# Shared experts of three steps as jobs among the first attention's rounds, in a two-layer decoder kernel

## The chip, the cores and the metric

The kernel runs as one program on one core of a Trainium2 chip. The engines of a core are TensorE (PE; its weight loads are shown apart, as PEld), VectorE (DVE), ScalarE (ACT), GpSimd (POOL) and SyncE (SP), which here only issues DMAs. Each engine takes its own instructions strictly in the order in which the program gives them, and engines wait for each other through semaphores. The metric is the device time of one execution in microseconds (us), the median of several executions. All data are float32; the trace shows two matmul records for each matmul of the program.

## The reference

Two decoder layers over `x` [4, 1024, 256], each with a mixing attention, a cross attention on 77 context rows and an expert feed-forward, with a layer norm after each. What matters here is the feed-forward of the first layer: 64 routed experts of width 64, of which each token takes 8, and two shared experts of width 512 that every token takes:

```python
def body(acc, p):                       # 64 routed experts
    W1, B1, W2, B2, e = p
    h = jax.nn.silu(xf @ W1 + B1) @ W2 + B2
    cw = jnp.sum(jnp.where(ti == e, tw, 0.0), axis=-1)
    return (acc + cw[:, None] * h, None)
routed, _ = jax.lax.scan(body, jnp.zeros_like(xf), (w1, b1, w2, b2, jnp.arange(w1.shape[0])))

def shared_mlp(W1, B1, W2, B2):         # 2 shared experts
    return jax.nn.silu(xf @ W1 + B1) @ W2 + B2
shared = jnp.sum(jax.vmap(shared_mlp)(sw1, sb1, sw2, sb2), axis=0)
return (routed + shared).reshape(b_, s_, d_)
```

## The kernel before

The program has four phases one after the other: the attention of layer 0, the feed (the feed-forward of layer 0), the attention of layer 1 and the gated feed-forward of layer 1. The sequence of 1024 tokens is cut into 8 steps; a step is 128 tokens of each of the 4 batch rows, so 512 tokens.

**The first attention** is a software pipeline of rounds. `SEQUENCE0` is a list of (stage, ahead, part), and in round n the stage works on step n - ahead. So round n does the retention of step n (`v`, `qk`, `kt`, `ret`, `mix`, `up`), the cross attention of step n - 1 (`wo`, `x1t`, `mx`, `mt`, `sc`, `pv`), the router of step n - 2 (`wout`, `x2t`, `rt`, `top`, `rank`) and the last things of step n - 3 (`cwt`, `b2`, and `put`, which scatters the rows of the step into the lists of their experts). Rounds 0 to 7 have the retention, round 8 has only the rest, and rounds 9 and 10 the tail. All engines go through the same list of jobs. A job of PE fills one of four narrow PSUM banks in turn, or the one wide bank of four (`ret`, `mx`, `sc`), and another engine empties it: `filled` and `emptied` are the waits. The stages `ret`, `mx` and `sc` share the one wide bank, so each of them waits until the one before was emptied.

**The shared experts** are cut into units. A step has `UNITS` = 8 units (1024 hidden columns by 128), so there are 64. A unit is `inward` (two matmuls of 512 columns, line 110), `activate` (Silu on ScalarE, line 118) and `outward` (four matmuls of 256 columns, line 127, which add up over the 8 units of a step). Units 0 to 7 stand in rounds 9 and 10 (`with_units`), all others in the feed.

**The feed** follows `feed_order`: first 20 units (`FIRST_UNITS`), then 80 quads of four expert pages each, with units between them. A quad loads 512 KB of rows from `lists`, PE transposes them (line 1716), multiplies by W1 (line 1728) and W2 (line 1739), and 512 KB go to `results`. The first 24 quads (`begun`) hold all pages of step 0. From quad 24 on there is a unit in four of five quads, and a `sum` in six of seven from the 26th on:

```python
units(0 if (j - begun) % 5 == 0 else 1)
if j >= begun + 2 and (j - begun) % 7:
    sums(1)
```

A `sum` n is `add_up` on DVE: it waits for gather n, four indirect DMAs of POOL (line 1441) that fetch the rows of one of the eight experts of a step, and adds them to the step. POOL runs gathers 0 to 48 one after the other within the feed, each with a `rest` instruction (line 158) ahead of it, and the other 15 in the second attention. DVE also copies the weights of the next quad (`stage`, lines 1633 and 1638), in the same order: the copy for quad 79 stands in quad 78, behind the sums of the quads before. The sums 46 to 48 stand ahead of all that DVE does in the second attention.

`base` adds the shared experts' result of a step to its residual rows, and `send` stores them; 8 steps, so 8 of each.

Of the kernel before, what the change touches and what calls it, by code (L numbers as in the profile page):

```python
# [11 lines left out]
P = 128  # L12
# [20 lines left out]
TOTAL = STEPS * UNITS  # L33
# [44 lines left out]
class SharedExperts:  # L78
# [16 lines left out]
    def load_rows(self, sp, src_t, s):  # L95
        for b in range(NB):
            at = b * SEQ + s * P
            sp.dma_start(self.sx[:, s % 2, :, b * P:(b + 1) * P],
                         src_t[:, at:at + P].rearrange("(c p) n -> p c n", p=P)).then_inc(self.sx_in[s % 2], 16)

    def inward(self, nc, pe, n, sp_h):
        s, u = n // UNITS, n % UNITS
        if n == 0:
            pe.wait_ge(self.sw1_in, 16 * ES)
# [16 lines left out]
    def outward(self, nc, pe, n, sp_y):  # L121
        u = n % UNITS
        if n == 0:
            pe.wait_ge(self.sw2_in, 16)
# [40 lines left out]
def steady(sequence):  # L165

    order = []
    for n in range(STEPS + max(ahead for _, ahead, _ in sequence)):
        for stage, ahead, part in sequence:
            if 0 <= n - ahead < STEPS:  # L170
                order.append((stage, n - ahead, part))
    return order
# [31 lines left out]
def bank_jobs(order):  # L204
# [5 lines left out]
    ("wout", 2, 0), ("wout", 2, 1), ("cwt", 3, 0), ("put", 3, 1), ("qk", 0, 0), ("x1t", 1, 0), ("x1t", 1, 1),  # L210
# [17 lines left out]
def attention_phase(nc, sems, shared, layer, d, src, src_t, dst, dst_t, experts, prefetch, lists, slots, weights, page_ends,  # L228
                    spare=None, route=None, block=None,
                    over=(), kept=(), late_on_pool=None, late_on_vector=None, units=None):  # L230
# [17 lines left out]
    with ExitStack() as ctx:  # L248
# [61 lines left out]
        if first:  # L310
# [25 lines left out]
            qt = x1t  # L336
        else:
# [49 lines left out]
        if first:  # L387
            cw_done = sem("cw_done")
            sent_cols = sem("sent_cols")
            sent_place, sent_cw = sem("sent_place"), sem("sent_cw")  # L390
            blank = [sem(f"blank{i}") for i in range(STEPS)]
        else:
            gate_exp = sem("gate_exp")
            sig_done = sem("sig_done")
            comb_done = sem("comb_done")
# [60 lines left out]
        def _(sp):  # L456
# [23 lines left out]
            prefetch(sp, 0)  # L480
            if first:
                sp.wait_ge(pool_ready, 3)
            out_rows = dst.rearrange("(b s) n -> s b n", b=NB)
            for n in range(STEPS + 3 if first else 0):
# [3 lines left out]
                if n == 1:  # L488
                    sp.dma_start(units.sb1[:], d["sb1"]).then_inc(units.sb1_in, 16)
                if 0 <= n - 3 < STEPS:  # L490
# [15 lines left out]
                if n + 2 < STEPS:  # L506
                    filled(sp, ("v", n, 1))
                    filled(sp, ("qk", n, 3))
                    load_t(n + 2)
                if n == STEPS - 1:  # L510
# [7 lines left out]
                    sp.wait_ge(sent_cols, 64 * 2)  # L518
                    for k in range(2):
                        units.load_rows(sp, dst_t, k)  # L520
                if 0 <= n - 2 < STEPS:
                    sp.wait_ge(cw_done, n - 1)
                    sp.dma_start(route[n - 2, 1], cw[:].rearrange("p b e -> p (b e)")).then_inc(sent_cw, 16)
                    sp.wait_ge(slot_done, n - 1)
                    sp.dma_start(route[n - 2, 0], place[:].rearrange("p b e -> p (b e)")).then_inc(sent_place, 16)
            for n in range(0 if first else STEPS + 3):
# [88 lines left out]
        def _(act):  # L615
# [71 lines left out]
        def _(dve):  # L687
# [83 lines left out]
            for job in order:  # L771
# [151 lines left out]
                if stage == "rank":  # L923
# [50 lines left out]
        def _(pe):  # L974
# [35 lines left out]
            for job in order:  # L1010
# [219 lines left out]
                if stage == "rank":  # L1230
# [6 lines left out]
                    fills(ins, job)  # L1237
                if stage == "cwt":
# [10 lines left out]
        if first:  # L1249
# [3 lines left out]
            over += [(blank[k], 16 * len(blanks(k))) for k in range(STEPS)]  # L1253
            return over, put_of[:2], (slot_done, STEPS)
# [13 lines left out]
def feed_order():  # L1268
# [33 lines left out]
    for j in range(QUADS0):  # L1302
# [7 lines left out]
        else:  # L1310
            weights(1)
            units(0 if (j - begun) % 5 == 0 else 1)
# [11 lines left out]
def feed_phase(nc, sems, shared_sems, d, w1, w_in, lists, page_ends, results, slots, weights, last_x2, last_slots, src, src_t, dst,  # L1324
# [9 lines left out]
    with ExitStack() as ctx:  # L1334
# [84 lines left out]
        def load_base(pool, s):  # L1419
            pool.wait_ge(base_sent, 16 * (s + 1))  # L1420
# [79 lines left out]
        def _(sp):  # L1500
# [9 lines left out]
            def load_rows(s):  # L1510
                if s:
                    sp.wait_ge(base_sent, 16 * s)
                sp.dma_start(base, by_step[s * P:(s + 1) * P]).then_inc(base_in, 16)

            def send_base(s):
                sp.wait_ge(sy_used, s + 1)
                sp.dma_start(out_by_step[s * P:(s + 1) * P], base).then_inc(base_sent, 16)
# [15 lines left out]
            for kind, n in order:  # L1533
# [14 lines left out]
                if kind == "unit" and n and n % UNITS == 0 and shared < STEPS:  # L1548
# [3 lines left out]
                if kind == "send":  # L1552
                    send_base(n)
                    if n + 1 < STEPS:
# [7 lines left out]
            sp.wait_ge(base_sent, 16 * STEPS)  # L1562
# [207 lines left out]
        over = [(sent[n], 16 * len(range(n, QUADS, NY))) for n in range(NY)] + [(base_sent, 16 * STEPS)]  # L1770
# [327 lines left out]
def decoder(nc, a, out):  # L2098
# [19 lines left out]
    with ExitStack() as ctx:  # L2118
# [24 lines left out]
        with nc.Block() as block:  # L2143
            over, put_before, placed = attention_phase(
                nc, sems, shared, 0, layer0, a["x"], a["x_t"], res1, res1_t, E0, load_layer0, lists0, slots0, weights0, page_ends0,
                halves[1], route0, block, units=experts)
# [78 lines left out]
```

## Time and profile before

| | before |
|---|---|
| median of 3 runs | 1869.29 us (1869.01 to 1887.16) |
| span of the profiled execution | 1981.9 us |
| mean granted TensorE clock | 0.922 of full |
| busy, PE / DVE / ACT / POOL | 1687.5 / 1165.2 / 623.2 / 892.7 us |
| chain that ended last | PE 68%, DVE 10%, issue 6%, DMA 6%, ACT 4%, POOL 3% |
| first attention, rounds 0 to 8 | until 558 us |
| rounds 9 and 10 and the first 20 units of the feed | 558 to 685 us |
| quads 0 to 23 | 685 to 777 us |
| quads 24 to 79 | 777 to 1105 us |
| second attention | from 1129 us |

The profiled execution took 1981.9 us from its first to its last instruction, 6.0% over the median of the runs without a profile. The busy times are of the profiled execution. A busy PE says that its matmuls stand close to each other, not that the array is at its peak; the granted clock is the share of 2.4 GHz that it was given, and it has two levels, full (1.0) and half (0.5, 1.2 GHz).

### The profile page before, as it was taken

What the parts mean: (1) busy time and instruction counts of PE and PEld (TensorE: products, weight loads), DVE (VectorE), ACT (ScalarE), POOL (GpSimd) and SP (SyncE); (2) the same over time, 40 slices, a digit from 0 to 9 for tenths busy, and PEclk for the clock granted to TensorE, in tenths of its full rate; (3) what the DMA queues carried; (4) which work ended last, traced back from release to release, by engine and by line L of the source; (5) the groups of instructions that cost most, each with busy time, mean ns of one, the idle gap of its engine ahead of it and who ended that gap; (6) DMA issues with size and microseconds to landing.
All of it is one profiled execution on the core that took longest, in us unless ns stands there. A gap on an engine that the chain in (4) does not pass through costs nothing.

```text
span 1981.9 us, 45543 instructions
## 1 busy us (share of the span) xinstructions
PE 1687.5 (85%) x17739; PEld 1329.8 (67%) x17739; DVE 1165.2 (59%) x3228; ACT 623.2 (31%) x957; POOL 892.7 (45%) x1000
## 2 busy tenths in 40 slices
PE   6788888887689889998998478889977599999994
PEld 4566665666566567666676355667666499999994
DVE  4576655665432177776656456788765245655564
ACT  1232322222231277454555223445432111111110
POOL 0017556655758102888888856333323102222223
PEclk9999989998689999999998779999987699999997
DMA  9416543555448899888998922113111512333332
GB/s 325 150 46 199 184 150 116 190 169 191 146 147 237 219 304 295 285 278 273 297 294 290 317 78 82 57 65 121 69 39 65 164 49 76 91 94 98 98 94 69
DMA packets 269634, 322.61 MB, mean 163 GB/s; under 512 B 25083, under 2 KB 245487, under 8 KB 268655
## 3 DMA queue, kind: packets, MB, share of 16 engines
q1 hardware_dynamic: 234559, 226.38, 36.1%
q0 software_dynamic: 33024, 92.32, 14.4%
q8 instruction: 144, 2.36, 0.5%
q10 hardware_dynamic: 1840, 1.00, 0.2%
q14 instruction: 67, 0.55, 0.1%
HBM read 157.22 MB, written 162.40 MB: 161 GB/s over the span
## 4 chain that ended last, share of the span: by engine, by line
PE 68%; DVE 10%; issue 6%; DMA 6%; ACT 4%; POOL 3%; another core or an unknown queue 2%; SPq 1%; DVEq 1%; POOLq 0%; ACTq 0%
PE wide L2067 13%; PE d_yp L2079 6%; PE wide L110 4%; PE wide L127 4%; PE wide L1199 4%; PE wide L1202 3%; PE wide L1728 3%; PE e_yp L1739 3%; PE wide L1186 3%; PE bank L1033 3%; PE bank L1212 3%; PE bank L1219 2%; PE e_xp L1716 2%; PE bank L1105 2%
## 5 line engine op out<-in xcount | busy, mean ns | idle before, releaser
L1441 POOL DMA_INDIRECT big<-results,slots x256 | 263.4, 1029 | 202.1 <-DMA results<-e_y 125.5
L2067 PE MATMUL wide<-d_xt,d_ws 128*128 128x128 f32 x2272 | 279.0, 277 | 0.6 <-issue 0.6
L2067 PEld LDWEIGHTS wide<-d_xt,d_ws 128*128 128x128 f32 x2272 | 272.7, 193 | 4.5 <-issue 1.0
L597 POOL DMA_INDIRECT lists<-big,slots x160 | 159.6, 997 | 116.7 <-DVE slots L961 70.3
L663 ACT ACTIVATE pt<-wide 77x2048 f32<-77x2048 f32 x64 | 119.8, 1871 | 196.5 <-PE wide L1202 118.7
L1936 POOL DMA_INDIRECT d_picked<-results,slots x64 | 64.0, 1001 | 182.0 <-DMA results<-d_y 168.7
L1967 ACT ACTIVATE d_gate<-wide 128x512 f32<-128x512 f32 x71 | 42.4, 597 | 323.9 <-PE wide L2067 323.9
L2079 PE MATMUL d_yp<-d_wd,d_h 128*128 x568 | 134.2, 379 | 0.0
L1456 DVE SCALAR_TENSOR_TENSOR big<-big,weights 128x256 f32<-128x256 f32 x256 | 108.9, 487 | 41.6 <-DMA big<-results,slots 28.2
L110 PE MATMUL wide<-shared_sx,shared_sw 128*128 128x512 f32 x256 | 126.3, 616 | 7.7 <-DMA shared_sx<-res_t 5.2
L127 PEld LDWEIGHTS wide<-shared_sw,shared_sh 128*128 128x128 f32 x512 | 97.3, 191 | 45.1 <-issue 29.6
L127 PE MATMUL wide<-shared_sw,shared_sh 128*128 128x256 f32 x512 | 121.4, 380 | 3.6 <-DVE big L1697 3.6
L158 POOL TENSOR_TENSOR rest_ones<-rest_ones 128x4 f32<-128x4 f32 x108 | 121.0, 1120 | 2.0
L554 POOL TENSOR_TENSOR rs<-mv,eps 128x4 f32<-128x4 f32 x32 | 6.4, 199 | 234.9 <-DVE mv L712 234.1
L1212 PE MATMUL bank<-pt,vals 77*32 77x128 f32 x2048 | 89.6, 293 | 25.3 <-issue 15.4
L2079 PEld LDWEIGHTS d_yp<-d_wd,d_h 128*128 128x128 f32 x568 | 102.6, 190 | 11.0
L1998 DVE COPY d_ws<-big 128x1024 f32 x142 | 92.3, 693 | 27.5 <-issue 26.4
L2016 DVE TENSOR_TENSOR d_h<-d_gate,wide 128x512 f32<-128x512 f32 x71 | 48.7, 686 | 97.7 <-PE wide L2067 97.7
L1587 ACT ACTIVATE e_xt<-e_xp 128x1024 f32<-128x1024 f32 x80 | 81.9, 1024 | 76.5 <-PE e_xp L1716 48.7
L1716 PE MATMUL e_xp<-e_ident,e_x 128*128 128x128 f32 x640 | 86.9, 280 | 15.8 <-DMA e_x<-lists 12.2
L1199 PE MATMUL wide<-x1t,keys 32*77 32x128 f32 x1024 | 69.7, 315 | 35.8 <-issue 13.6
L1728 PE MATMUL wide<-e_xt,e_w1s 128*64 128x128 f32 x1280 | 89.4, 283 | 12.5 <-DVE e_w1s L1633 11.0
(280 smaller groups left out, 3488.8 us busy)
## 6 DMA issues: line engine op xcount, KB each, us to landing
lists<-zero SPq DMA_DIRECT2D x20, 2048.0 KB, 14.6
e_x<-lists SPq DMA_DIRECT2D x80, 512.0 KB
results<-e_y SPq DMA_DIRECT2D x80, 512.0 KB
d_x<-lists SPq DMA_DIRECT2D x71, 128.0 KB
results<-d_y SPq DMA_DIRECT2D x71, 128.0 KB
e_w<-in_L_w SPq DMA_DIRECT2D x2, 4096.0 KB
shared_sw<-in_x_t SPq DMA_DIRECT2D x32, 128.0 KB
x<-in_x SPq DMA_DIRECT2D x8, 512.0 KB
```

What stands on the lines that cost most here:

```text
L110: ins = nc.tensor.matmul(sp_h, self.sw1[:, c, u * P:(u + 1) * P], self.sx[:, s % 2, c], start=c == 0, stop=c == KC - 1)
L127: ins = nc.tensor.matmul(sp_y[b // 2][:, b % 2 * DM:(b % 2 + 1) * DM], self.sh[:, n % 2, b * P:(b + 1) * P], self.sw2[:, u], start=u == 0 ...
L158: step(self.nc.gpsimd.tensor_tensor(self.ones[:, 1], self.ones[:, 0], self.ones[:, 0], ALU.pow))
L597: pool.indirect_dma_start(out=lists, out_offset=bass.IndirectOffsetOnAxis(ap=slots[:, b, i, k:k + 1], axis=0), in_=z2[i % 3][:, b, :], in_ ...
L663: empties(nc.scalar.activation(pt[0:CTX, p % 2].rearrange("k (j n) -> k j n", j=4), ps[0:CTX], ACT.Exp, scale=score_scale), job)
L1199: mm(out[0:CTX, r, n * P:(n + 1) * P], keys[quarter(r), p, c, h * CTX:(h + 1) * CTX], qt[quarter(r), c, toks(p)], start=True, stop=False, ...
L1212: ins = mm(out[quarter(r), at:at + P], vals[:, p, c * 8 + 2 * r + h], pt[0:CTX, p % 2, of:of + P], start=True, stop=True)
L1441: pool.indirect_dma_start(out=picked[:, c % NG, b, :], out_offset=None, in_=results[0:-(-PAGES_OF_STEP[s] // 4) * 4 * R0, :], in_offset=ba ...
L1716: ins = tr(xp[:, h, (a * KC + c) * P:(a * KC + c + 1) * P], x[:, j % NX, h, a, c * P:(c + 1) * P], ident[:])
L1728: ins = mm(hp[h * H0:(h + 1) * H0, a * R0:(a + 1) * R0], w1s[:, j % NW1, h, a, c], xt[:, j % 2, h, a, c], start=c == 0, stop=c == KC - 1)
L2067: ins = mm(out[T % 2][:, a * P:(a + 1) * P], ws[:, T % NW, n, c, a * P:(a + 1) * P], xt[:, T % 2, c], start=c == 0, stop=c == KC - 1)
L2079: ins = mm(yp[T % 2][:, 0:DM], h[:, T % 2, c * P:(c + 1) * P], wd_flat[:, bass.ds(e * (HC * DM) + c * DM, DM)], start=c == 0, stop=c == HC ...
```

## The change

The shared experts of steps 0 to 2 (`SOON` = 3), 24 of the 64 units, become jobs of the first attention. A step is two groups of four units (`FOUR`); group i stands in round i + 3, so rounds 3 to 8 have one group each. A group is four jobs `win` (two matmuls of 512 columns each on PE; Silu on ScalarE) and two jobs `wtwo` (eight matmuls of 256 columns each on PE, which add up over the four units; DVE adds the bank to the residual rows `gbase`). The jobs use the narrow banks. The feed and `with_units` work on the other five steps, with 40 units: 8 in rounds 9 and 10, 20 at the start of the feed as before, and 13 instead of 37 between the quads, one in four quads.

```diff
+SOON = 3
+FOUR = UNITS // 2
+GROUPS = SOON * UNITS // FOUR
+TOTAL = (STEPS - SOON) * UNITS
...
-    ("wout", 2, 0), ("wout", 2, 1), ("cwt", 3, 0), ("put", 3, 1), ("qk", 0, 0), ("x1t", 1, 0), ("x1t", 1, 1),
+    ("wout", 2, 0), ("wout", 2, 1), ("cwt", 3, 0), ("put", 3, 1), ("win", 3, 0), ("qk", 0, 0), ("x1t", 1, 0), ("x1t", 1, 1),
...
-            units(0 if (j - begun) % 5 == 0 else 1)
+            units(0 if (j - begun) % 4 else 1)
...
+                if stage == "win":
+                    u, at = i % 2 * FOUR + p, i % 2 * FOUR + p
+                    if i == 0 and p == 0:
+                        act.wait_ge(units.sb1_in, 16)
+                    if i >= 2 and p == 0:
+                        filled(act, ("wtwo", i - 2, 1))
+                    ps = filled(act, job)
+                    empties(nc.scalar.activation(gh[:, at], ps[:], ACT.Silu, bias=units.sb1[:, u:u + 1]), job)
...
+                if stage == "wtwo":
+                    pair = slice(2 * p, 2 * p + 2)
+                    dve.wait_ge(gbase_in, 16 * (i // 2 + 1))
+                    ps = filled(dve, job)
+                    if i % 2:
+                        emptied(dve, ("wtwo", i - 1, p))
+                    ins = nc.vector.tensor_tensor(gbase[:, pair], ps[:].rearrange("p (b n) -> p b n", b=2),
+                                                  gbase[:, pair], ALU.add)
+                    empties(ins, job)
...
+                if stage == "win":
+                    u = i % 2 * FOUR + p
+                    if i == 0 and p == 0:
+                        pe.wait_ge(units.sw1_in, 16 * ES)
+                        pe.wait_ge(units.sw2_in, 16)
+                    if i % 2 == 0 and p == 0:
+                        pe.wait_ge(gx_in, 64 * (i // 2 + 1))
+                    for c in range(KC):
+                        ins = mm(out[:], gw1[:, c, u * P:(u + 1) * P], gx[:, c], start=c == 0, stop=c == KC - 1)
+                    fills(ins, job)
+                if stage == "wtwo":
+                    for n in range(FOUR):
+                        emptied(pe, ("win", i, n))
+                    for bb in range(2):
+                        for n in range(FOUR):
+                            u = i % 2 * FOUR + n
+                            ins = mm(out[:, bb * DM:(bb + 1) * DM], gh[:, u, toks(2 * p + bb)], gw2[:, u],
+                                     start=n == 0, stop=n == FOUR - 1)
+                    fills(ins, job)
```

On SP's queue the change adds, in the first attention: the shared experts' weights a second time, into the half of `big` that later holds the feed's W1 (in round 1, 2 MB), the step's columns `gx` (512 KB in rounds 2, 4 and 6, after the wait for `sent_cols`), the residual rows `gbase` (512 KB in rounds 3, 5 and 7, after the wait for `sent_rows`) and their store into `mid` (rounds 4, 6 and 8, after `wtwo` was emptied). The load of the feed's W1 (`prefetch`, 4 MB) moves from the start of the kernel to the end of round 8, and the first rows of the units in the tail from round 7 to round 8. The feed has 5 bases, 5 sends and 3 loads of unit rows where it had 8, 8 and 6. POOL's instructions are the same; only its wait for the stored base falls away for the first three steps.

In PE's order of round 6, from the transposed router weights (`cwt`) to `b2`, there stands before:

```order
L1241 MATMUL bank_0<-ident,cw 64x128 x4
L1033 MATMUL bank_0<-shared_sw,wqk 128x512 x2
L1105 MATMUL bank_0<-ident,x 128x128 x8
L1186 MATMUL wide<-keys,x1t 128x154 x8
L1033 MATMUL bank_0<-shared_sw,wqk 128x512 x2
L1246 MATMUL bank_0<-b_0,cwt 128x256 x4
```

and in the changed kernel:

```order
L1327 MATMUL bank_0<-ident,cw 64x128 x4
L1313 MATMUL bank_0<-big 128x512 x2
L1100 MATMUL bank_0<-shared_sw,wqk 128x512 x2
L1172 MATMUL bank_0<-ident,x 128x128 x8
L1253 MATMUL wide<-keys,x1t 128x154 x8
L1100 MATMUL bank_0<-shared_sw,wqk 128x512 x2
L1313 MATMUL bank_0<-big 128x512 x2
L1332 MATMUL bank_0<-b_0,cwt 128x256 x4
```

The first `win` stands ahead of the first `qk`, the second behind the second `qk`; the third stands behind the third `mx` and the fourth ahead of the first `kt`. Later in the same round, from the last matmuls of `mix` 0 over `ret` 1 (wide) and `pv` 0 to `sc` 1, before:

```order
L1074 MATMUL bank_0<-big,shared_sx 32x128 x4
L1057 MATMUL wide<-shared_sw 128x128 x16
L1212 MATMUL bank_0<-pt,vals 32x128 x16
L1199 MATMUL wide<-x1t,keys 77x128 x4
L1202 MATMUL wide<-shared_sh,sel 77x128 x4
```

and in the changed kernel:

```order
L1141 MATMUL bank_0<-big,shared_sx 32x128 x4
L1124 MATMUL wide<-shared_sw 128x128 x16
L1279 MATMUL bank_0<-pt,vals 32x128 x16
L1321 MATMUL bank_0<-big 128x256 x8
L1266 MATMUL wide<-x1t,keys 77x128 x4
L1269 MATMUL wide<-shared_sh,sel 77x128 x4
```

The second `wtwo` stands between `pv` 0 and `sc` 1; the first one stands in the same way between `sc` 0 and `mix` 0. On ScalarE, the same round, from `cwt` to the exponential of the router, in the changed kernel (before there is neither a Silu nor a table load in it):

```order
L667 ACTIVATE cwt<-bank_0 64x512
L687 ACT_TABLE_LOAD
L687 ACTIVATE big<-bank_0,shared_sb 128x512
L667 ACTIVATE x1t<-bank_0 128x2x2x128 x2
L740 ACTIVATE big<-big,rs 128x256 x4
L687 ACTIVATE big<-bank_0,shared_sb 128x512
L667 ACTIVATE x2t<-bank_0 128x2x2x128 x2
L687 ACTIVATE big<-bank_0,shared_sb 128x512 x2
L667 ACTIVATE shared_sx<-bank_0 128x512 x2
L667 ACTIVATE shared_sh<-bank_0 128x512
L725 ACT_TABLE_LOAD
L725 ACTIVATE ex<-lg 128x256
```

Silu and the exponential lie in different tables, so each of rounds 3 to 8 has two loads of a table on ScalarE, 12 in all.

## Rows read from the trace of the kernel before

**Rows 1.** The page: span, and the granted clock in 40 slices

```profile
span 1981.9 us, 45543 instructions
PEclk9999989998689999999998779999987699999997
```

**Rows 2.** Busy time by stretch: round 6, round 8, first units, quads in three stretches

```profile
core 0: us, PE busy (x) PEld busy (x) DVE busy (x) ACT busy (x) POOL busy (x), PEclk, DMA share, GB/s
350.50:417.80 67.30, 56.76 (x835) 42.96 (x831) 41.55 (x104) 18.67 (x25) 40.39 (x46) 0.92 0.48 156
485.00:558.40 73.40, 53.10 (x537) 39.78 (x534) 34.24 (x98) 15.40 (x19) 47.10 (x52) 0.68 0.61 202
600.40:685.20 84.80, 75.14 (x257) 48.28 (x255) 12.66 (x37) 14.43 (x21) 43.74 (x46) 0.96 0.89 233
685.20:776.60 91.40, 81.78 (x832) 62.47 (x832) 65.77 (x219) 67.65 (x103) 0.00 (x0) 1.00 0.92 294
776.60:1059.40 282.80, 268.88 (x1877) 191.21 (x1873) 183.66 (x599) 141.74 (x216) 229.31 (x219) 0.99 0.88 283
1059.40:1105.00 45.60, 34.79 (x298) 26.25 (x296) 30.74 (x110) 23.45 (x37) 37.57 (x37) 0.89 0.91 297
```

**Rows 3.** PE in order of time, units at the start of the feed

```profile
614.25 1.88 PE L110 MATMUL wide<-shared_sx,shared_sw 128*128 128x512 f32 x4
615.96 1.89 PE L127 MATMUL wide<-shared_sw,shared_sh 128*128 128x256 f32 x8
617.69 1.88 PE L110 MATMUL wide<-shared_sx,shared_sw 128*128 128x512 f32 x4
```

**Rows 4.** Waits of PE in round 6: us in total, times, longest

```profile
PE wide L1199 <- issue: 2.3, 3, 1.7
PE wide L1057 <- issue: 1.5, 2, 0.9
...
PE wide L1199 <- DVE big L788: 1.1, 1, 1.1
PE bank L1212 <- ACT pt L663: 1.1, 1, 1.1
```

**Rows 5.** Waits of PE in round 8

```profile
PE bank L1105 <- ACT x L674: 4.2, 2, 3.8
PE wide L1199 <- ACT pt L663: 3.4, 1, 3.4
...
PE bank L1212 <- ACT pt L663: 2.2, 2, 2.1
PE bank L1192 <- DVE shared_sh L854: 1.9, 1, 1.9
PE wide L1186 <- DVE shared_sh L854: 1.6, 1, 1.6
```

**Rows 6.** Waits of POOL from 780 to 1128 us

```profile
POOL big L1441 <- issue: 46.0, 151, 0.3
POOL big L1441 <- POOL rest_ones L158: 14.1, 49, 0.3
POOL big L1441 <- DVE big L1456: 0.3, 1, 0.3
```

**Rows 7.** POOL in order of time: two puts of four, gathers 0 and 48

```profile
631.59 1.04 POOL L1572 DMA_INDIRECT lists<-big,slots  x1 [0.29 <-POOL rest_ones L158]
...
637.77 1.04 POOL L1572 DMA_INDIRECT lists<-big,slots  x1 [0.29 <-POOL rest_ones L158]
...
780.61 0.99 POOL L1441 DMA_INDIRECT big<-results,slots  x1 [125.49 <-DMA results<-e_y]
...
1113.07 1.01 POOL L1441 DMA_INDIRECT big<-results,slots  x1 [0.29 <-POOL rest_ones L158]
```

**Rows 8.** DVE in order of time: sums 44 and 48, start of the second attention

```profile
1095.55 1.67 DVE L1456 SCALAR_TENSOR_TENSOR big<-big,weights 128x256 f32<-128x256 f32 x4 [2.14 <-issue]
...
1125.96 1.67 DVE L1456 SCALAR_TENSOR_TENSOR big<-big,weights 128x256 f32<-128x256 f32 x4 [5.36 <-DMA big<-mid]
1127.64 0.28 DVE L722 MEMSET state<- 128x260 f32 x1
```

**Rows 9.** ScalarE at the first unit, a load of the table and a Silu

```profile
566.20 1.28 ACT L118 ACT_TABLE_LOAD   x1 [9.80 <-PE wide L110]
567.50 0.69 ACT L118 ACTIVATE shared_sh<-wide,shared_sb 128x512 f32<-128x512 f32 x1
```

More of the change, by code:

```diff
@@ L169, in steady @@
         for stage, ahead, part in sequence:
-            if 0 <= n - ahead < STEPS:
+            if 0 <= n - ahead < (GROUPS if stage in ("win", "wtwo") else STEPS):
                 order.append((stage, n - ahead, part))
@@ L209 @@
     ("wo", 1, 0), ("wo", 1, 1), ("put", 3, 0), ("v", 0, 0), ("v", 0, 1), ("ln1", 1, 0),
-    ("wout", 2, 0), ("wout", 2, 1), ("cwt", 3, 0), ("put", 3, 1), ("qk", 0, 0), ("x1t", 1, 0), ("x1t", 1, 1),
[4 rows of a table removed]
+    ("wout", 2, 0), ("wout", 2, 1), ("cwt", 3, 0), ("put", 3, 1), ("win", 3, 0), ("qk", 0, 0), ("x1t", 1, 0), ("x1t", 1, 1),
+    ("mx", 1, 0), ("ln2", 2, 0), ("qk", 0, 1), ("win", 3, 1), ("b2", 3, 0), ("b2", 3, 1), ("mx", 1, 1), ("res", 1, 0), ("put", 3, 2),
+    ("qk", 0, 2), ("x2t", 2, 0), ("x2t", 2, 1), ("mx", 1, 2), ("win", 3, 2), ("put", 3, 3), ("qk", 0, 3), ("mx", 1, 3), ("put", 3, 4),
+    ("win", 3, 3), ("kt", 0, 0), ("ret", 0, 0), ("kt", 0, 1), ("put", 3, 5), ("mt", 1, 0), ("rt", 2, 0), ("put", 3, 6), ("put", 3, 7),
+    ("sc", 1, 0), ("wtwo", 3, 0), ("mix", 0, 0), ("top", 2, 0), ("ret", 0, 1), ("pv", 1, 0), ("wtwo", 3, 1), ("sc", 1, 1),
+    ("mix", 0, 1), ("up", 0, 0),
     ("rank", 2, 0), ("sc", 1, 2), ("pv", 1, 1), ("sc", 1, 3), ("pv", 1, 2), ("pv", 1, 3),
@@ L229, in attention_phase @@
                     spare=None, route=None, block=None,
-                    over=(), kept=(), late_on_pool=None, late_on_vector=None, units=None):
+                    over=(), kept=(), late_on_pool=None, late_on_vector=None, units=None, soon_memory=None, mid=None):
     first = layer == 0
@@ L479, in _, with load_group, load_gbase, send_gbase @@
             load_t(1)
-            prefetch(sp, 0)
             if first:
                 sp.wait_ge(pool_ready, 3)
+            else:
+                prefetch(sp, 0)
             out_rows = dst.rearrange("(b s) n -> s b n", b=NB)
+            def load_group(s):
+                for b in range(NB):
+                    at = b * SEQ + s * P
+                    sp.dma_start(gx[:, :, b * P:(b + 1) * P],
+                                 dst_t[:, at:at + P].rearrange("(c p) n -> p c n", p=P)).then_inc(gx_in, 16)
+            def load_gbase(s):
+                sp.wait_ge(sent_rows[0], 16 * (s + 1))
+                if s:
+                    sp.wait_ge(gbase_sent, 16 * s)
+                else:
+                    sp.wait_ge(ready, READY)
+                sp.dma_start(gbase, out_rows[s * P:(s + 1) * P]).then_inc(gbase_in, 16)
+            def send_gbase(s):
+                for p in range(2):
+                    emptied(sp, ("wtwo", 2 * s + 1, p))
+                sp.dma_start(mid.rearrange("(b s) n -> s b n", b=NB)[s * P:(s + 1) * P], gbase)\
+                    .then_inc(gbase_sent, 16)
             for n in range(STEPS + 3 if first else 0):
@@ L489, in _ @@
                     sp.dma_start(units.sb1[:], d["sb1"]).then_inc(units.sb1_in, 16)
+                    sp.dma_start(gw2, d["sw2"].rearrange("e (c p) n -> p (e c) n", p=P)).then_inc(units.sw2_in, 16)
+                    for e in range(ES):
+                        sp.dma_start(gw1[:, :, e * HS:(e + 1) * HS], d["sw1"][e].rearrange("(c p) n -> p c n", p=P))\
+                            .then_inc(units.sw1_in, 16)
                 if 0 <= n - 3 < STEPS:
@@ L509, in _ @@
                     load_t(n + 2)
+                if n >= 2 and n % 2 == 0 and n // 2 - 1 < SOON:
+                    s = n // 2 - 1
+                    if s:
+                        filled(sp, ("win", 2 * s - 1, FOUR - 1))
+                    sp.wait_ge(sent_cols, 64 * (s + 1))
+                    load_group(s)
+                if n >= 3 and n % 2 == 1 and (n - 3) // 2 < SOON:
+                    load_gbase((n - 3) // 2)
                 if n == STEPS - 1:
@@ L525, in _ @@
                     sp.dma_start(route[n - 2, 0], place[:].rearrange("p b e -> p (b e)")).then_inc(sent_place, 16)
+                if n >= 4 and n % 2 == 0 and n // 2 - 2 < SOON:
+                    send_gbase(n // 2 - 2)
+                    if n // 2 - 2 == SOON - 1:
+                        filled(sp, ("wtwo", GROUPS - 1, 1))
+                        prefetch(sp, 0)
             for n in range(0 if first else STEPS + 3):
@@ L1547, in _ @@
                     load_route((n + 1) // 6)
-                if kind == "unit" and n and n % UNITS == 0 and shared < STEPS:
+                if kind == "unit" and n and n % UNITS == 0 and SOON + shared < STEPS:
                     sp.wait_ge(experts.full, n)
@@ L1769, in feed_phase @@
         kept = [(stored[s % NA], 16 * (s // NA + 1)) for s in range(STEPS)]
-        over = [(sent[n], 16 * len(range(n, QUADS, NY))) for n in range(NY)] + [(base_sent, 16 * STEPS)]
+        over = [(sent[n], 16 * len(range(n, QUADS, NY))) for n in range(NY)] + [(base_sent, 16 * (STEPS - SOON))]
         return over, kept, late_on_pool, late_on_vector
```

30 lines of the change are left out of this document (19 added, 11 removed), and 4 rows, old and new, of the table SEQUENCE0.

## The prediction

> **What bounds the kernel now.** I read the busy times by stretch first, since the change takes work out of one stage and puts it into another, and then in each of the two stages which wait ends last. In the first attention a middle round takes 67.3 us and PE is busy for 56.8 of them; DVE has 41.6, POOL 40.4 and ACT 18.7 [rows 2]. The waits of PE in that round are many and small, the longest 1.7 us [rows 4]. So a round is as long as PE's own work with some 10 us of holes, of which only few are places where a foreign job would stand. Round 8 is different: no retention, 73.4 us long, PE busy for 53.1, clock 0.68 [rows 2], and waits of 4.2, 3.4, 2.2, 1.9 and 1.6 us on ACT and DVE [rows 5]. Round 8 follows from chains, and PE has room in it.
>
> In the feed the reader is to look at POOL, though PE is busier. From 776.6 to 1059.4 us PE is busy for 268.9 of 282.8 us [rows 2], which by itself says that PE bounds it. But POOL, whose busy time is only 229.3, has not one real wait in the whole stretch: its waits are 46.0 us before indirect DMAs and 14.1 us behind its own rest instruction, all of 0.3 us each, and a single 0.3 us for DVE [rows 6]. So POOL goes at its own pace from gather 0 at 780.61 to gather 48 at 1113.07 [rows 7], 332.5 us for 48 gathers, 6.93 us each. And the end of the feed hangs on it: DVE stood still for 2.14 us before sum 44 (which the program's order places ahead of the copies for the last quads) and for 5.36 us before sum 48 (on the residual rows, whose load POOL issues behind gather 48), and the second attention's first DVE instruction comes right behind that, at 1127.64 [rows 8]. From 1059.4 on, without a unit in the way, PE is busy for only 34.8 of 45.6 us [rows 2]: there the quads already follow POOL.
>
> **The change part by part.** *PE work put into the rounds.* A unit in full stride takes 617.69 - 614.25 = 3.44 us [rows 3], so a group of four 13.8 us, and six groups 82.6 us. The matmuls are the same in number and shape as in the feed.
>
> *Rounds 3 to 7.* What fills holes: the fourth `win` stands ahead of the first `ret`, and the first `wtwo` ahead of `mix` 0 and so of the second `ret`; the two waits of line 1057 (1.5 us) go. The second `wtwo` stands ahead of `sc` 1; the longest wait of line 1199 (1.7 us) goes [rows 4]. The waits of 1.1 us at the first `sc` and the last `pv` have no new job ahead of them and stay. That hides 3.2 us. Then the clock: 0.92 over 67.3 us [rows 2] means 16% of the round at half speed, 10.8 us, which would have taken 5.4 us at full speed. No trace shows what denser work does to it. The ends: all is given back (growth 13.8 - 3.2 - 5.4 = 5.2 us a round), or the half-speed stretch stays and one `wtwo` pair of 3.4 us falls into it and takes twice as long (13.8 - 3.2 + 3.4 = 14.0 us). I take 2 us given back, nearer to nothing than to all, because the jobs stand at two points of a stretch whose other matmuls stay as they are: 8.6 us a round, 43 us for five rounds, with ends of 26 and 70.
>
> *Round 8.* The first `win` stands ahead of the transposes that wait 4.2 us, the third ahead of the last `mx` (1.6), the fourth ahead of `mt` (1.9), the first `wtwo` ahead of `pv` 0 (2.2) [rows 5]: 9.9 of 13.8 us are hidden. The 3.9 left I set against the clock, which was at half speed for 64% of the round: 0, with ends of -10 and +8.
>
> *ScalarE and VectorE in the rounds.* 24 Silus of 0.69 us and 12 table loads of 1.28 us [rows 9] are 32 us, 5.3 a round on an engine that has 18.7 of 67.3 busy [rows 2]; the copies of `x1t` are queued behind the first Silu and PE's `mx` waits for them, but a `qk` of two 512-column matmuls and eight transposes lie between. The second table load lies ahead of the exponentials, for which the first `wtwo` gives PE 3.4 us of other work. Two DVE adds of about 0.7 us (as line 1456 takes 1.67 for four of half the size [rows 8]) lie in an idle DVE; `top` and `pv` are queued behind them, and PE has `mix` and `sc` to do meanwhile. I take 0; if each round showed the table load and the Silu once it would be 6 x 2.0 = 12 us.
>
> *SP's queue.* The waits for `sent_cols` and `sent_rows` stand ahead of the route stores, which wait for later work anyway; the wait for `wtwo` stands ahead of the next round's clears of the lists. The 4 MB load of W1 now lies at the end of round 8 instead of at the start. The DMA engines are 0.61 busy in round 8 [rows 2], and W1 is not needed before the first quad at 685 us; at 283 GB/s [rows 2] it takes 15 us. What can be late is the clear of the last part of the lists behind it. I take 0, with ends of -3 (the start is rid of it) and +8.
>
> *The feed.* 24 x 3.44 = 82.6 us of PE work go out of quads 24 to 79, three bases and sends with them. The first 20 units stay, and quads 0 to 23 (91.4 us, no units, DMA engines 0.92 busy [rows 2]) stay. What is late next is POOL, which is late already. Its pace could rise if less contends with it: two puts of four with their rest are 637.77 - 631.59 = 6.18 us apart [rows 7], so 48 gathers at that pace would take 297 us, 36 less than now; but every eighth gather also has a load, a store and two norm instructions on POOL, some 3 us, 18 us in all, which leaves 18 at most. The routed traffic of the quads and gathers, which fills the DMA engines to 0.88, is unchanged, so I take -3, with ends of 0 and -18.
>
> Sum: 43 + 0 + 0 + 0 - 3 = +40 us on the profiled 1981.9 us [rows 1], so 2022. The runs without a profile are at 1869.29, 0.943 of that, and the same share of the 40 is 38: 1907 us.
>
> **The rivals.** *The rounds swallow the jobs.* The granted clock is 1.00 where work stands dense (quads 0 to 23) and 0.92 and 0.68 in the rounds [rows 2]. If the added dense matmuls hold it at full speed, rounds 3 to 7 grow by 26 us, round 8 shrinks by 10 and the feed gives 3: +13 us, 1881. The Trainium skill (TensorE: Matmul & The Clock Gate, "What's actually happening") says that the default state is throttled and that activity releases the throttle; by that rule this rival wins, and the trace agrees in part, for round 8 has the lowest clock and the most idle PE. Against it speaks that the dips in rounds 3 to 7 lie where PE is 84% busy.
>
> *The feed gives PE's time back.* If POOL only looks busy because it is paced by the quads, quads 24 to 79 shrink by up to 82.6 us, and the kernel ends at 1981.9 + 43 - 83 = 1942, which is 1832 without a profile. For it speaks PE's 268.9 of 282.8; against it that POOL has no wait for sums or results. It comes out ahead by 1% only if gathers come every 6.93 - (43 + 20) / 48 = 5.6 us, less than the 6.18 that POOL needs where nothing disturbs it.
>
> *The rounds pay in full.* Half-speed stretches stay, the jobs run into them, table loads show, the last clear is late: 70 + 8 + 12 + 8 = 98 us, with the feed's 3 it is 95, 1959 us.
>
> **How the numbers follow.** Likeliest case 0.56 (its own range 1888 to 1930), the rounds swallow it 0.20, the feed gives back 0.09, pay in full 0.15. The range reaches from the second case with the feed's larger end (26 - 10 - 18 = -2, so 1867) to inside the last: 1867 to 1948. About 1% is what a measurement of this kernel can tell from no change, so 1850.6 and 1888.0 are the limits: faster 0.09, no difference 0.21 (the second case and the edge of the first), slower 0.70.
>
> **What would show it.** Right: rounds 3 to 7 some 76 us long each (67.3 before) and round 8 near 73; first gather of POOL late by the attention's growth; from there 332 us again to gather 48, still without waits, while PE is busy for about 190 of the 283 us and its clock falls there; the second attention and the gated phase unchanged in length. Wrong in the first step: rounds of 72 us or less at a clock of 1.0. Wrong in the last: gathers closer than 6.5 us. Also wrong if DVE waits for `gbase` in a round, or if the feed starts late behind W1.

## Result and the profile after

The changed kernel takes 1920.56 us (median of 4 runs, 1915.56 to 1922.53), the kernel before 1871.61 us: a ratio of 1.0256 with a 95% interval of 1.022 to 1.0293, so it is 2.6% slower. The forecast was 1907, range 1867 to 1948.

The first profile of the kernel before [rows 1 to 9] turned out to be of a disturbed execution: a second one (e1, below) has a span of 1866.4 us, close to its runs, so e1 stands for before from here on. Against e1 the first profile is 80.1 us longer up to the end of POOL's last put, 5.8 from there to quad 0 and 30.6 behind gather 48, all ahead of the gated feed-forward (421 us in both); from quad 0 to gather 48 it is 1.1 us shorter.

The page of e1, span and granted clock in 40 slices:

```profile
span 1866.4 us, 45543 instructions
...
PEclk9999999997999999999997689899985999999997
```

The page of the changed kernel:

```profile
span 1920.2 us, 45608 instructions
...
PEclk9999999999999898888998679999996899999997
```

The clock digits of the first attention (slices 1 to 11) are 9 in both but for one 7 in e1 (round 8), where [rows 1] have a 6 and two 8s. A 9 stands for anything from 0.90 on, so whether a round has 0.92 or 1.00 is read from the stretches below. By places that both traces have (the first `mx` of a round, POOL's last put, the first quad, the last gather of the feed), in us:

| stretch | before (e1) | after | difference |
|---|---|---|---|
| start to `mx` of round 3 | 162.4 | 161.0 | -1.4 |
| `mx` of round 3 to `mx` of round 8 | 273.3 | 323.5 | +50.2 |
| from there to the end of the last put | 139.1 | 138.0 | -1.1 |
| last put to quad 0 | 24.5 | 29.3 | +4.8 |
| quad 0 to gather 48 | 429.0 | 431.6 | +2.6 |
| gather 48 to the end | 838.2 | 836.8 | -1.4 |

The sum is 53.7 us between the two profiled executions, 49 between the medians. Rounds 3 to 7 hold nearly all of it. The other differences are about what executions of the same program differ by: from the last put to quad 0, for one, the changed kernel takes 29.3 us here, 26.2 in e4 and 26.7 in e9, whose programs are the same there but for the Silu of e4, and the kernel before 24.5 in e1, 26.5 in e12 and 29.4 in e10.

Busy time by stretch of e1, as in [rows 2]: round 5, quads 0 to 23, and gather 0 to quad 72. (The 91.4 us in [rows 2] run past quad 24, which begins at 767.4 us there; quads 0 to 23 take 82.2 us in both profiles.)

```profile
core 0: us, PE busy (x) PEld busy (x) DVE busy (x) ACT busy (x) POOL busy (x), PEclk, DMA share, GB/s
269.60:324.00 54.40, 48.59 (x832) 38.44 (x831) 41.88 (x104) 18.89 (x25) 39.93 (x46) 1.00 0.60 200
...
599.30:681.50 82.20, 72.48 (x736) 55.26 (x736) 57.73 (x191) 59.80 (x91) 0.00 (x0) 1.00 0.91 292
...
694.20:980.00 285.80, 274.01 (x1944) 196.32 (x1942) 190.15 (x611) 149.95 (x224) 235.69 (x223) 0.99 0.89 287
```

The same of the changed kernel, up to quad 77:

```profile
core 0: us, PE busy (x) PEld busy (x) DVE busy (x) ACT busy (x) POOL busy (x), PEclk, DMA share, GB/s
287.50:352.30 64.80, 62.40 (x880) 47.32 (x879) 42.83 (x105) 23.98 (x31) 40.86 (x46) 1.00 0.57 185
...
651.80:734.70 82.90, 74.20 (x738) 56.28 (x736) 59.77 (x198) 59.93 (x91) 0.00 (x0) 0.98 0.92 292
...
747.70:1050.00 302.30, 224.44 (x1762) 165.28 (x1762) 198.67 (x652) 140.71 (x213) 249.21 (x235) 0.87 0.84 273
```

The reader is to see two things. A round gained 62.40 - 48.59 = 13.81 us of PE work and became 10.4 us longer; its holes shrank from 5.81 to 2.40 us, and the clock was full in both. In the feed PE went from 274.0 of 285.8 us to 224.4 of 302.3, and the time from gather 0 to gather 48 did not shrink. In e1 and in the changed kernel (POOL in order of time, start and us, as in [rows 7]):

```profile
694.20 0.99 POOL L1441 DMA_INDIRECT big<-results,slots  x1 [119.23 <-DMA results<-e_y]
...
1028.25 1.01 POOL L1441 DMA_INDIRECT big<-results,slots  x1 [0.29 <-POOL rest_ones L158]
```

```profile
747.67 0.99 POOL L1529 DMA_INDIRECT big<-results,slots  x1 [124.97 <-DMA results<-e_y]
...
1083.37 1.01 POOL L1529 DMA_INDIRECT big<-results,slots  x1 [0.29 <-POOL rest_ones L161]
```

That is 334.1 and 335.7 us. Which holes were filled, the waits of PE show, as [rows 4] did. In e1's round 5 (us in total, times, longest):

```profile
PE wide L1199 <- DVE big L788: 2.4, 1, 2.4
PE bank L1212 <- ACT pt L663: 1.1, 1, 1.1
PE wide L1199 <- ACT pt L663: 1.0, 1, 1.0
PE wide L1057 <- DVE shared_sh L854: 0.8, 1, 0.8
PE wide L1186 <- ACT x1t L617: 0.3, 1, 0.3
```

and in the changed kernel's round 5:

```profile
PE bank L1279 <- ACT pt L721: 1.1, 1, 1.1
PE wide L1266 <- ACT pt L721: 1.0, 1, 1.0
PE wide L1253 <- ACT x1t L667: 0.3, 1, 0.3
```

The 2.4 us ahead of `sc` 1 (line 1199) and the 0.8 us ahead of `ret` (line 1057) are gone, 3.2 us; the other three stand as they were.

### The profile page after: what moved, and what is told of

The parts are those of the page before. It is cut to its first block, busy times and chain, and to the rows that moved or that the text cites. A ratio compares the mean times of both kernels' runs of the same rounds, so it can differ in the third digit from the quotient of the medians.

```text
span 1920.2 us, 45608 instructions
## 1 busy us (share of the span) xinstructions
PE 1631.4 (85%) x17739; PEld 1300.8 (68%) x17739; DVE 1171.6 (61%) x3234; ACT 639.4 (33%) x969; POOL 898.5 (47%) x1000
## 4 chain that ended last, share of the span: by engine, by line
PE 59%; POOL 18%; issue 7%; DVE 7%; DMA 5%; ACT 4%; SPq 1%; DVEq 0%; POOLq 0%; ACTq 0%
PE wide L2155 13%; POOL big L1529 11%; PE d_yp L2167 6%; POOL rest_ones L161 3%; PE bank L1100 3%; PE wide L1266 3%; PE wide L1269 2%; PE bank L1286 2%; PE bank L1313 2%; PE bank L1321 2%; PE wide L1253 2%; PE wide L113 2%; PE wide L130 2%; ACT pt L721 2%; PE bank L1279 2%
## 5 line engine op out<-in xcount | busy, mean ns | idle before, releaser
L1816 PE MATMUL wide<-e_xt,e_w1s 128*64 128x128 f32 x1280 | 99.5, 304 | 81.0 <-DVE e_w1s L1721 80.8
L1816 PEld LDWEIGHTS wide<-e_xt,e_w1s 128*64 128x64 f32 x1280 | 77.8, 151 | 96.9 <-DVE e_w1s L1721 89.1
L1827 PE MATMUL e_yp<-e_w2s,e_ht 64*128 64x256 f32 x640 | 105.1, 453 | 1.3 <-ACT e_y L1675 1.3
L1804 PE MATMUL e_xp<-e_ident,e_x 128*128 128x128 f32 x640 | 89.2, 284 | 13.1 <-DMA e_x<-lists 11.5
L1675 ACT ACTIVATE e_y<-e_yp 128x1024 f32<-128x1024 f32 x80 | 81.9, 1024 | 54.6 <-PE e_yp L1827 54.6
L1804 PEld LDWEIGHTS e_xp<-e_ident,e_x 128*128 128x128 f32 x640 | 71.9, 144 | 39.3 <-DMA e_x<-lists 20.4
L658 POOL DMA_INDIRECT lists<-shared_sw,slots x64 | 62.4, 975 | 70.0 <-PE wide L1269 30.4
```

Source lines behind the costliest of these rows:

```text
L1675: return nc.scalar.activation(out, in_, ACT.Copy)
L1804: ins = tr(xp[:, h, (a * KC + c) * P:(a * KC + c + 1) * P], x[:, j % NX, h, a, c * P:(c + 1) * P], ident[:])
L1816: ins = mm(hp[h * H0:(h + 1) * H0, a * R0:(a + 1) * R0], w1s[:, j % NW1, h, a, c], xt[:, j % 2, h, a, c], start=c == 0, stop=c == KC - 1)
L1827: ins = mm(yp[:, h, a * DM:(a + 1) * DM], ht[lanes, j % 2, a], w2s[lanes, j % NW2, a, 0:DM], start=True, stop=True)
```

## The experiments

Three theories. A, the prediction's: the rounds pay for the jobs, since PE bounds them, and the feed gives next to nothing back, since POOL paces it. B: the feed does give PE's time back, 30 us or more, and the rounds pay 80. C: the added loads, stores and waits on SP's queue pay part of it.

**e1, the kernel before again.** No edit.

> The kernel before, unchanged, for a second profile: the span of the first one (1981.9 us) lies 6% over its runs without a profile, while the span of the changed kernel (1920.2 us) lies at its runs. If the recording itself costs 6%, the span is near 1980 again. If the first profile held stretches that most executions don't have, the span is near 1870, the gathers of the feed keep their pace of 6.9 us, and the rounds of the first attention are shorter than 67.3 us: near 57 if theory A is right (each round pays some 8 us for its group; the changed kernel's are 64.8).

The span was 1866.4 us, and the second case holds: the rounds are 54.4 us long, not 67.3. The recording itself costs nothing that shows. The clock of 0.92 explains 5.4 of the 12.9 us by which a round of the first profile is longer. Most of the rest shows as waits of PE that nothing in the profile ends ("issue"), mostly between its matmuls of 32 rows or 32 columns: 31.7 us from round 3 to round 7 in the first profile (148.2 to 485 us), 0.9 us in e1 (148.2 to 433 us). What caused them is open.

**e2, no jobs.** `win` and `wtwo` leave the list; SP waits for its own loads instead.

```diff
-    ("sc", 1, 0), ("wtwo", 3, 0), ("mix", 0, 0), ("top", 2, 0), ("ret", 0, 1), ("pv", 1, 0), ("wtwo", 3, 1), ("sc", 1, 1),
+    ("sc", 1, 0), ("mix", 0, 0), ("top", 2, 0), ("ret", 0, 1), ("pv", 1, 0), ("sc", 1, 1),
...
-                    emptied(sp, ("wtwo", 2 * s + 1, p))
+                sp.wait_ge(gbase_in, 16 * (s + 1))
```

> The changed kernel with the jobs win and wtwo left out on PE, ScalarE and VectorE (the shared experts of steps 0 to 2 are computed nowhere); its loads and stores, the place of the load of W1 and the short feed stay. Theory A (the rounds pay, the feed is paced by POOL and gives some 3 us back): 1865 to 1872 us, at the kernel before or up to 5 us under it. Theory B (the feed gives 30 us or more back and the rounds pay 80): 1840 or less. Theory C (the new loads, stores and waits on SP pay part of the 49 us): 1885 or more.

1874.06 us, ratio to before 0.9998 (0.9979 to 1.0018). With the loads, the stores, the late W1 and the short feed all in place the kernel is as fast as before: the 49 us are the jobs, and C falls as an explanation of them. A's 1865 to 1872 was missed by 2 us. C is not nothing, though, as e3 shows.

**e3, the short feed alone.**

```diff
-TOTAL = STEPS * UNITS
+SOON = 3
+TOTAL = (STEPS - SOON) * UNITS
...
-            units(0 if (j - begun) % 5 == 0 else 1)
+            units(0 if (j - begun) % 4 else 1)
```

> The kernel before with the changed kernel's short feed: 24 units left out between the quads (the shared experts of steps 0 to 2 are computed nowhere), nothing else moved. What the feed alone gives back. Theory A: 0 to 5 us under the kernel before, gathers again 6.8 to 6.9 us apart and without waits. Theory B: 30 us or more under it, gathers 6.2 us apart or less.

1866.96 us, ratio 0.9949 (0.9932 to 0.9965), 7 us under before by the medians and 10 by the ratio. 82.6 us of PE work are gone, and 7 to 10 us come back. B falls, and A's 0 to 5 was too little. Gather 0 to gather 48 takes 335.0 us, no less than before:

```profile
698.76 0.99 POOL L1444 DMA_INDIRECT big<-results,slots  x1 [123.29 <-DMA results<-e_y]
...
1033.78 1.01 POOL L1444 DMA_INDIRECT big<-results,slots  x1 [0.29 <-POOL rest_ones L159]
```

Where the 7 us lie the profiles don't tell; the profiled execution of e3 was the slowest of its four. Neither e2 nor e3 has the jobs, both have the short feed, and what e2 has beyond e3 are the loads, the stores, their waits and the late W1. It is 7 us slower (1874.06 against 1866.96), and the two intervals don't overlap: C's part costs about what the short feed gives back. In which stretch is not shown.

**e4, no table loads.**

```diff
-gh[:, at], ps[:], ACT.Silu, bias=units.sb1[:, u:u + 1]
+gh[:, at], ps[:], ACT.Identity, bias=units.sb1[:, u:u + 1]
```

> The changed kernel with Identity in place of Silu for the jobs win (so the result of the shared experts of steps 0 to 2 is another one), which takes the 12 table loads out of rounds 3 to 8. If ScalarE's table loads lie beside other work, as the prediction took it: 1915 to 1921 us, within 5 us of the changed kernel. If each round shows its table load and a Silu: 12 us less, near 1908.

1916.81 us, ratio 1.0231 (1.0208 to 1.0254), which overlaps the changed kernel's interval. The rounds are the same to 0.1 us; round 5 of e4:

```profile
290.70:355.50 64.80, 62.40 (x880) 47.33 (x879) 42.86 (x105) 21.40 (x29) 40.82 (x46) 1.00 0.56 183
```

ScalarE is busy for 21.40 instead of 23.98 us, and nobody notices: its work lies beside PE's. The feed is the changed kernel's, and its gathers 0 to 48 take 331.4 us here and 335.7 there: single profiles of the same code differ by 4 us in that stretch.

**e5, fewer units ahead of the first quad, in the changed kernel.**

```diff
-FIRST_UNITS = 20
+FIRST_UNITS = 12
...
-            units(0 if (j - begun) % 4 else 1)
+            units(1 if (j - begun) % 5 in (1, 3) else 0)
```

> The changed kernel with 12 instead of 20 units ahead of the first quad and 20 instead of 13 between quads 24 to 79 (two in five). If the feed is paced by POOL and has PE time to spare since the change (in the changed kernel PE is busy for 73 to 79 of each 100 us there), the eight units cost nothing between the quads, and the first quad follows the last put of POOL after some 8 us instead of 29: about 20 us less than the changed kernel, near 1900. If PE's time in the feed still counts, the 27 us only move: near 1920.

1919.56 us, ratio 1.0254 (1.0214 to 1.0295): nothing. The first quad began at 641.54 instead of 651.82 us, 10 us earlier and not 20, and PE stood still for 23.8 us ahead of it. SP's queue in order of time (start, us) shows why:

```profile
602.25 24.27 SPq L101 DMA_DIRECT2D shared_sx<-res_t  x4
626.56 2.17 SPq L1605 DMA_DIRECT2D mid<-big  x1
636.02 0.36 SPq L1601 DMA_DIRECT2D big<-res  x1
636.49 7.38 SPq L1592 DMA_DIRECT2D e_x<-lists  x4
```

The rows of the first quad (`e_x`) are queued behind the next `base` load, and that waits until the stored base has landed, 9 us. POOL's last put had ended at 623.8. Of the 10 us that were gained, 4 are left at the end of the profile: the gathers took 339.9 instead of 335.7 us and quads 0 to 23 1.6 us more, both within what single profiles of the same code differ by. The medians show 1.

**e6, the same in the kernel before**, with `units(1 if j % 8 == 7 else 0)` for quads 0 to 23.

> The kernel before with the same 12 units ahead of the first quad, three units between quads 0 to 23 and 44 between the others. Here PE has less room: in the second profile of the kernel before it is busy for 103.2 of 105.8, 92.6 of 100 and 78.2 of 80 us between gather 0 and quad 72. If POOL alone paces the feed: 16 to 20 us under the kernel before. If PE is a close second, as those numbers say, the gathers go some 2 to 4% slower (7.1 us apart) and half or more of it is lost: 5 to 10 us under.

1878.04 us, ratio 1.0029 (0.9998 to 1.006): a miss. Quad 0 starts 11.5 us earlier than in e1 (587.8 against 599.3), but quads 0 to 23 with three units take 91.5 instead of 82.2 us, and the gathers 339.9 instead of 334.1:

```profile
587.80:679.30 91.50, 84.09 (x760) 63.72 (x760) 58.24 (x190) 61.31 (x93) 0.00 (x0) 0.94 0.82 263
...
694.40:980.00 285.60, 275.96 (x1917) 196.31 (x1916) 187.12 (x606) 147.66 (x222) 236.28 (x218) 0.99 0.90 289
```

Before the change PE is a close second limit in the feed. In quads 0 to 23 the three units of 3.44 us show nearly in full (9.3 us); of the five more among the gathers, 17.2 us of PE work, 5.8 us show.

**e7, one step, its groups in rounds 7 and 8**, 12 units ahead of the first quad.

```diff
-SOON = 3
+SOON = 1
...
-    ("win", 3, 3), ("kt", 0, 0), ("ret", 0, 0), ("kt", 0, 1), ("put", 3, 5), ("mt", 1, 0), ("rt", 2, 0), ("put", 3, 6), ("put", 3, 7),
+    ("win", 7, 3), ("kt", 0, 0), ("ret", 0, 0), ("kt", 0, 1), ("put", 3, 5), ("mt", 1, 0), ("rt", 2, 0), ("put", 3, 6), ("put", 3, 7),
```

> The changed kernel with one step instead of three (SOON = 1), its two groups in rounds 7 and 8, and 12 units ahead of the first quad, so that the eight units come out of the stretch that bounds the first quad. By the readings so far a group costs 10.4 us in a round with retention (64.8 against 54.4 us) and nothing in round 8: 10.4 - 20 = 10 us under the kernel before, near 1864. If round 8 was free only by chance of the long rounds ahead of it: near 1874.

1875.41 us, ratio 1.002 (0.9995 to 1.0044): no gain, and a miss. From `cwt` of round 7, which stands ahead of the first job, to the end of the last put it takes 206.6 us (196.8 in e1), 9.8 us for two groups, as 10.4 and nothing would give. The time fits the other case of the expectation, near 1874, but its reason doesn't hold: from `mx` of round 8 to the last put it takes 138.3 us, and 139.1 in e1, so round 8 is free here too. The gain at the first quad is missing for e5's reason: PE waited 25.9 us for `e_x`, whose load followed that of the `base` at 599.05 us.

**e8, one step, both groups in round 8.** The list is rewritten so that `win` and `wtwo` of both groups stand in round 8 alone.

> As the one ahead, but both groups stand in round 8, which has no retention. PE is busy for 58.8 of the 73 us from round 8's start in the second profile of before, at a clock of 0.86, so there are some 14 us of holes and a group is 13.8 us: the first is free, the second costs between 0 and 13.8 us there. 1854 to 1868; under the one ahead if the holes take more than 3 us of the second group, which is what a round with retention takes.

1879.36 us, ratio 1.0044 (1.0019 to 1.0068), slower than before: a miss. Round 8 did what was expected of it, for the last put ends 5.8 us later than in e1 (580.66 against 574.82) with 27.6 us of PE work more. But PE then waits for SP's queue:

```profile
602.86 1.51 PE L1804 MATMUL e_xp<-e_ident,e_x 128*128 128x128 f32 x6 [24.17 <-DMA e_x<-lists]
```

**e9 and e10, half of POOL's rests**, in the changed kernel and in the kernel before.

```diff
-            if c:
+            if c and (c % 2 or c >= LATE):
                 shared_sems.rest(pool)
```

> The changed kernel, with POOL's rest instruction ahead of every second of the gathers 1 to 45 instead of ahead of every one (23 rests of some 1.33 us with their wait fall away, 31 us). If POOL's own pace sets the feed (theory A): gathers 6.3 instead of 7.0 us apart, 25 to 31 us less than the changed kernel, 1890 to 1895. If the gathers only look busy and go at the pace of the quads, of DVE or of the DMA engines: they wait in other places, the time stays at 1915 to 1921.

> The same in the kernel before, where PE is busy for 274 of the 285.8 us from gather 0 to quad 72. Theory A with PE as the second limit: PE's time holds the gathers back, so it gains only what PE has spare and the part after the last unit, 8 to 16 us under the kernel before, 1856 to 1864, and the distance to the changed kernel with the same edit shrinks from 49 to some 35 us. If PE had been no limit at all: 25 to 31 us under, 1841 to 1847, and the distance stays. If POOL is not the limit: no change.

e9: 1896.56 us, ratio 1.0155 (1.0096 to 1.0215), 24 us under the changed kernel by the medians and 2 above its range (the rests taken away are 22, not 23: 29 us). Gather 0 to gather 48 takes 310.6 us, 25.1 less:

```profile
743.80 0.99 POOL L1529 DMA_INDIRECT big<-results,slots  x1 [120.04 <-DMA results<-e_y]
...
1054.40 1.01 POOL L1529 DMA_INDIRECT big<-results,slots  x1 [0.29 <-POOL rest_ones L161]
```

e10: 1863.06 us, ratio 0.9944 (0.9918 to 0.997). Gather 0 to gather 48 takes 321.5 us, only 12.5 less, and POOL now waits (us in total, times, longest):

```profile
POOL big L1441 <- issue: 53.2, 164, 3.8
POOL big L1441 <- POOL rest_ones L158: 6.9, 24, 0.3
POOL mid L1417 <- DVE big L1477: 6.1, 2, 4.5
POOL big L1441 <- DVE big L1456: 5.6, 2, 5.3
```

Waits of 5.3 and 4.5 us for DVE's sums and norms stand where [rows 6] have none over 0.3. Both halves of A are shown by this pair: POOL's own instructions set the feed, and the PE time that the change takes out becomes worth something (12 us here) when POOL goes faster. That PE stands behind DVE's delay in e10 is an inference, from PE's 274.5 of 281.8 us between gather 0 and 980 us. The distance between the kernels falls from 49 to 33.5 us.

**e11 and e12, a third of the rests**: e11 with e8's round 8, 20 units ahead of the first quad and 28 between the quads (`units((j - begun) % 2)`); e12 is the kernel before with nothing else.

```diff
-            if c:
+            if c and (c % 3 == 0 or c >= LATE):
                 shared_sems.rest(pool)
```

> A version meant to beat both: one step (SOON = 1) as two groups in round 8 as in e8, 20 units ahead of the first quad as before, 28 between the quads (every second), and a rest ahead of every third of the gathers 1 to 45 (30 rests fewer, 40 us). Round 8 costs 6 us by e8's profile, PE in the feed has nine units or 31 us less to do than before. If POOL's pace sets the feed as long as PE has time: gathers 6.1 us apart, 6 - 38 = 32 us under the kernel before, near 1838, with PE near full. If the gathers have a third limit (DVE's sums, landing): 1850 to 1863, no better than e10.

> The kernel before with the same third of the rests, no unit moved. If PE already bounds the feed of e10 (gathers 6.7 us apart, PE busy for 278.7 of 286 us): nothing more is gained, 1860 to 1866, and the units moved to round 8 in e11 are worth the difference, some 25 us. If it gains as much as e11 (under 1845), PE is not the limit and moving units is worth nothing even with a faster POOL.

e11: 1863.78 us, ratio 0.995 (0.9918 to 0.9982); 1838 was a miss. e12: 1856.31 us, ratio 0.9897 (0.9865 to 0.9928), the fastest kernel of all and 4 us under its range. In e11 the gathers go as expected, 299.2 us from the first row to the second, 6.2 us each, and POOL's longest wait among them is 0.3 us:

```profile
714.43 0.99 POOL L1529 DMA_INDIRECT big<-results,slots  x1 [130.06 <-DMA results<-e_y]
...
1013.58 1.01 POOL L1529 DMA_INDIRECT big<-results,slots  x1 [0.29 <-POOL rest_ones L161]
```

In e12 they take 319.7 us, hardly less than in e10, with PE at 273.2 of 281.3 us:

```profile
698.70:980.00 281.30, 273.23 (x1935) 195.60 (x1933) 189.81 (x618) 148.99 (x223) 208.21 (x201) 0.99 0.90 293
```

So the units moved out do buy 20.5 us in the gathers. They are lost on both sides of them. Quad 0 of e11 starts at 615.6 us, that of e12 at 603.0 (7.7 us of it in the attention, the rest behind the last put). And the end of the gathers no longer decides: gather 48 starts 4.8 us earlier in e11, but PE begins the second attention 7.7 us later, at 1039.01 against 1031.28 us, having waited 24.9 us (22.3 in e12) for constants that SP loads behind the last quad's store. In e11 that store is late because of the units, of which the last still stand behind the last quad:

```profile
1007.60 1.14 PE L1827 MATMUL e_yp<-e_w2s,e_ht 64*128 64x256 f32 x8 [1.27 <-ACT e_y L1675]
1008.67 1.98 PE L113 MATMUL wide<-shared_sx,shared_sw 128*128 128x512 f32 x4
1010.49 3.62 PE L130 MATMUL wide<-shared_sw,shared_sh 128*128 128x256 f32 x16
```

DVE waits 9.9 us for them before the last `base`, SP 7.7 us for DVE before it stores that base, and the last quad's store is queued behind it: the second attention's first load starts at 1021.08 us, in e12 at 1015.98, though the last quad's last matmuls start at 1007.60 and 1007.89. From gather 0 to 980 us the DMA engines are busy at a share of 0.96:

```profile
714.40:980.00 265.60, 243.72 (x1824) 176.56 (x1823) 193.29 (x639) 143.18 (x217) 213.09 (x205) 0.95 0.96 313
```

Why e12 is 7 us under e10, whose gathers take as long, is open; their intervals overlap.

## Why the prediction held, point by point

**The rounds are bound by PE and pay** (right, mis-sized). 13.8 us of PE work a group and 3.2 us of filled holes, as forecast: 13.81 and 3.2 were measured. The holes are at the two places that were named, but that their sum agrees is luck: 1.7 us ahead of `sc` 1 and 1.5 ahead of `ret` in the disturbed profile are 2.4 and 0.8 in e1. The step that was off is the clock: 2 us a round were to be given back, because the first profile showed 0.92. In e1 and in the changed kernel the clock is 1.00 in round 5, so there was nothing to give back, and a round grew by 10.4 us, not 8.6: 50 instead of 43. For the same reason the prediction's own sign of a wrong first step came, rounds of 72 us or less at a clock of 1.0 (64.8 at 1.00), without the step being wrong: the rounds before are not 67.3 us long but 54.4.

**Round 8 costs nothing** (right): -1.1 us from its `mx` to the last put.

**ScalarE, VectorE and SP cost nothing in the rounds** (right): e4 for the table loads, e2 for the loads and stores (its round 5 takes 54.5 us), and no wait of DVE for `gbase` in any round. Over the whole kernel SP's part was taken as 0, with ends of -3 and +8, and e2 against e3 puts it at some 7. The Trainium skill (ScalarE: Activation LUTs, "What ACT_TABLE_LOAD costs") gives 2.66 us for a switch, 1.28 of load and 1.38 of drain. This trace shows the load alone: in round 4 the instruction ahead of it ends at 221.73 us, the load starts at 221.75 and takes 1.28, and the Silu follows at 223.04. That it doesn't count for the time e4 shows.

**The feed is paced by POOL and gives 3 us back** (right in kind). The profiles show +2.6 from quad 0 to gather 48, which is no clear difference, e3 by its runs -7. PE was to be busy for some 190 of 283 us; from gather 0 to gather 48 it was busy for 239.2 us instead of 301.0, only 61.8 less for 82.6 us of work taken out, since the clock fell from 0.99 to 0.87, as forecast. The first quad is 4.8 us later behind the last put, which the sum had at 0: PE waited 6.8 us for the rows of a unit there (2.0 in e1), behind SP's queue. Other executions of both kernels differ by as much there.

**From the profile to the median** (wrong): the sum was multiplied by 0.943, as if those 6% lay everywhere. They lay nearly all in the two attentions. In hindsight, without that factor and the clock term the same working gives 5 x (13.8 - 3.2) - 3 = 50 us, 1919 on the median it started from; the measured time is 1920.56.

**The rivals.** That the rounds swallow the jobs fell with the full clock of e1. That the feed gives PE's time back fell with e3, and its condition (gathers under 5.6 us apart) was never met, not even with a third of the rests (6.2). That the rounds pay in full came nearest, but its half-speed stretches and table loads are not there.

## What to carry to other kernels

A busy engine is not the pace of a stage. In this feed PE was 96% busy and POOL 82%, yet taking 82.6 us from PE gave 7 to 10 us back, and taking 29 us from POOL (22 rests of 1.33) gave 24: look for the engine that has no wait, however its busy time reads. Before work is moved, ask of both places what bounds them; here it went from under POOL's cover into the one stage that PE did bound. And compare a profile's span with the unprofiled runs by stage before a sum is scaled from one to the other.

## What the runs showed of the hardware

The clock of TensorE dropped where its work became thinner. From gather 0 on it was at 0.99 with PE busy for 274 of 285.8 us, and at 0.87, so in part at the lower level of 1.2 GHz, with 224 of 302.3; nobody waited for that, since POOL set the pace. Dips also come without any difference in the program: e10 and e12 differ in the rests of the feed alone, and round 6 took 54.5 us at 1.00 in the one and 57.1 at 0.94 in the other:

```profile
325.00:379.50 54.50, 48.69 (x833) 38.55 (x832) 41.81 (x103) 18.89 (x25) 40.05 (x46) 1.00 0.60 197
323.40:380.50 57.10, 51.29 (x832) 40.89 (x832) 41.99 (x103) 18.38 (x25) 39.20 (x46) 0.94 0.54 181
```

When both POOL and PE were relieved in e11, the 16 DMA engines were busy at a share of 0.96 and moved 313 GB/s, against 0.89 and 287 in e1. In e1 PE at 96% and the DMA engines at 0.89 stood close behind POOL. Taking 29 us from POOL gave 25 us in the gathers where PE had been relieved (e9) and 12.5 where it had not (e10).
